# Query-bias products of a 16-head cross-attention layer: four 32-column groups and a spread through DRAM in place of a repeated 128-column weight

## The reference

```python
def _cross_attention(q_in, kv_in, wq, bq, wk, bk, wv, bv, wo, bo, bias_k, bias_v):
    b, q_len, _ = q_in.shape
    t = kv_in.shape[1]
    qh = (q_in @ wq + bq).reshape(b, q_len, H, K)
    kh = (kv_in @ wk + bk).reshape(b, t, H, K)
    vh = (kv_in @ wv + bv).reshape(b, t, H, K)
    kh = jnp.concatenate([kh, jnp.broadcast_to(bias_k, (b, 1, H, K))], axis=1)
    vh = jnp.concatenate([vh, jnp.broadcast_to(bias_v, (b, 1, H, K))], axis=1)
    scale = jnp.sqrt(jnp.asarray(K, q_in.dtype))
    logits = jnp.einsum('bqhk,bthk->bhqt', qh, kh) / scale
    weights = jax.nn.softmax(logits, axis=-1)
    ctx = jnp.einsum('bhqt,bthk->bqhk', weights, vh).reshape(b, q_len, H * K)
    return ctx @ wo + bo
```

## Time and profile before

| what | value |
|---|---|
| median of three runs | 795.99 us |
| the profiled execution | 796.76 us, of which its span is 794.8 us |
| PE busy | 697.0 us, 88% of the span |
| DVE, ACT, POOL busy | 492.8, 319.8, 318.4 us |
| chain that ended last | PE 61%, DVE 20%, DMA 5%, ACT 4%, POOL 4% |
| DMA moved | 46.70 MB, mean 59 GB/s |

### The profile page before, as it was taken

One profiled execution on the slowest core, in us unless ns is written; L12 is line 12 of the kernel. 1 busy time (PEld: TensorE's weight loads), 2 busy tenths in 40 slices (PEclk: granted clock), 3 DMA queues, 4 the chain that ended last, 5 costly groups with the idle time before them and its releaser, 6 DMA issues.

```text
span 794.8 us, 11731 instructions
## 1 busy us (share of the span) xinstructions
PE 697.0 (88%) x4432; PEld 509.8 (64%) x4432; DVE 492.8 (62%) x840; ACT 319.8 (40%) x693; POOL 318.4 (40%) x292
## 2 busy tenths in 40 slices
PE   6769989778978897699999999999998998795798
PEld 5446655447864454487757777875767897254588
DVE  4356677656555999546457674334797766498553
ACT  2044444423204777455532225652332411486311
POOL 4023444521524888453126640002675522286200
PEclk9578998999989999899999999999999999998899
DMA  5866742010006000004530000440000002000000
GB/s 174 226 161 187 215 116 46 2 35 0 1 1 211 1 1 1 2 22 163 188 106 1 1 1 19 148 152 1 0 1 1 1 1 92 15 1 1 0 27 27
DMA packets 40528, 46.70 MB, mean 59 GB/s; under 512 B 5697, under 2 KB 34970, under 8 KB 40346
## 3 DMA queue, kind: packets, MB, share of 16 engines
q1 hardware_dynamic: 38888, 44.46, 18.6%
q10 hardware_dynamic: 1586, 1.51, 0.7%
HBM read 37.72 MB, written 8.13 MB: 58 GB/s over the span
## 4 chain that ended last, share of the span: by engine, by line
PE 61%; DVE 20%; DMA 5%; ACT 4%; POOL 4%; issue 3%; ACTq 1%; SPq 1%; DVEq 0%; POOLq 0%
PE narrow_ps L510 8%; PE wide_ps L852 7%; PE wide_ps L491 6%; PE narrow_ps L887 5%; PE wide_ps L803 5%; PE wide_ps L839 3%; PE wide_ps L826 3%; PE wide_ps L543 3%; PE narrow_ps L693 3%; DVE scoresb L1376 3%; DVE mx L1385 2%; DMA wstream<-in_wqT 2%; PE wide_ps L471 2%; DVE sums L1392 2%; POOL probs L1684 2%
## 5 line engine op out<-in xcount | busy, mean ns | idle before, releaser
L1675 POOL TENSOR_TENSOR scoresb<-scoresb,mx 128x768 f32<-128x768 f32 (+1 forms) x40 | 70.7, 1769 | 152.5 <-DVE mx L1383 114.5
L1661 POOL TENSOR_TENSOR rstd<-veps,mhalf 128x1 f32<-128x1 f32 x56 | 33.2, 593 | 146.6 <-DVE veps L1304 146.6
L1051 ACT ACTIVATE probsT<-wide_ps 128x1024 f32<-128x1024 f32 x40 | 41.0, 1025 | 103.1 <-PE wide_ps L543 103.1
L1684 POOL TENSOR_TENSOR probs<-scoresb,rcp 128x1024 f32<-128x1024 f32 x40 | 78.2, 1955 | 7.0 <-DVE rcp L1393 7.0
L510 PE MATMUL narrow_ps<-wstream_r,hidden 128*128 128x256 f32 x576 | 71.9, 285 | 8.0 <-DVE hidden L1361 7.7
L510 PEld LDWEIGHTS narrow_ps<-wstream_r,hidden 128*128 128x128 f32 x576 | 70.8, 191 | 9.5 <-DVE hidden L1361 8.2
L491 PE MATMUL wide_ps<-xq_r,wstream_r 128*128 128x512 f32 x192 | 64.7, 419 | 4.8 <-issue 4.5
L543 PEld LDWEIGHTS wide_ps<-ident,probs 128*128 128x128 f32 x320 | 38.0, 146 | 46.5 <-issue 45.9
L543 PE MATMUL wide_ps<-ident,probs 128*128 128x128 f32 x320 | 44.3, 284 | 25.1 <-POOL probs L1684 23.3
L1444 DVE TENSOR_REDUCE mx<-wide_ps 128x2 f32<-128x640 f32 x64 | 49.6, 818 | 18.6 <-PE wide_ps L629 18.1
L803 PE MATMUL wide_ps<-scoresb_r,probs_r 128*128 128x256 f32 x256 | 55.7, 300 | 6.1 <-DVE vwb L1550 4.2
(11 more groups left out here) (182 smaller groups left out, 1526.3 us busy)
## 6 DMA issues: line engine op xcount, KB each, us to landing
wstream<-in_L_xattn_wk SPq DMA_DIRECT2D x8, 512.0 KB, 3.9
wstream<-in_L_xattn_wv SPq DMA_DIRECT2D x8, 512.0 KB, 5.1
wstream<-in_L_xattn_wo SPq DMA_DIRECT2D x8, 512.0 KB, 6.2
wstream<-in_wqT SPq DMA_DIRECT2D x8, 512.0 KB, 7.7
qrow<-qscratch SPq DMA_DIRECT2D x16, 192.0 KB
kscratch<-kparts SPq DMA_DIRECT2D x7, 320.0 KB, 2.4
qscratch<-qparts SPq DMA_DIRECT2D x8, 256.0 KB, 2.9
wstream<-in_L_xattn_mlp_w SPq DMA_DIRECT2D x2, 1024.0 KB, 5.3
```

The costliest lines, as they stand in the source:

```text
L1051: nc.scalar.activation(dst, src, ACT.Identity, **kw).then_inc(ring.drained[ring.slot(key)], 1)
L1675: g.tensor_tensor(s3[:, first:], s3[:, first:], mx[:, u % 3, first:].unsqueeze(2).broadcast_to([P, 16 - first, n_scores]), ALU.subtract).t ...
L1684: g.tensor_tensor(probs[:, u % 2, :].rearrange("p (h k) -> p h k", h=16), s3[:, :, 0:T], rcp[:, u % 3, :].unsqueeze(2).broadcast_to([P, 16 ...
```

## The change

The product bq times keys is issued once for a pair of heads, in the odd head, as four matmuls whose weights have 32 equal columns. Column group i (output rows 32i to 32i + 31) holds half of the keys (129 of 257, one key twice) of one head. ACT scales the 129 columns into a small row buffer. SP then stores one row of each group to DRAM (two DMAs, two rows of 129 numbers each), waits until both have landed, and loads the 514 numbers of the pair from DRAM into all 128 rows of cB with one DMA. SP does that for two pairs ahead of each weight group from g = 2 on, and for four pairs ahead of the load of the MLP's weights. DVE waits at the start of `attend2` for all eight loads in place of ACT's last two scalings. The row buffers are two; ACT waits for the store of two pairs before.

```diff
-                    bq = column(f"L2_bq{a + 1}", h)
-                    ps, filled = take_narrow(("cB", a, h))
-                    mm(ps[:, 0:NK2], bq.broadcast_to([P, P]), hb[:, 0:NK2], start=True, stop=True).then_inc(filled, 1)
-
                     if h % 2 == 1:
+                        ps, filled = take_narrow(("cB", a, h // 2))
+                        for i in range(4):
+                            g, lo = h - 1 + i // 2, i % 2 * (NK2 - HALF_KEYS)
+                            m = mm(ps[32 * i:32 * i + 32, 0:HALF_KEYS], column(f"L2_bq{a + 1}", g).broadcast_to([P, 32]),
+                                   heads[g % 4][:, lo:lo + HALF_KEYS], start=True, stop=True)
+                        m.then_inc(filled, 1)
...
+            def score_bias(a, pair):
+
+                n = 8 * a + pair
+                sp.wait_ge(*narrow.empty(("cB", a, pair)))
+                for i in range(2):
+                    lo, hi = (0, NK2 - HALF_KEYS) if i == 0 else (NK2 - HALF_KEYS, NK2)
+                    sp.dma_start(cscratch[a, 2 * pair:2 * pair + 2, lo:hi],
+                                 cbrow[n % 2][32 * i:32 * i + 65:64, 0:hi - lo]).then_inc(cb_stored[n % 2], 16)
+                sp.wait_ge(cb_stored[n % 2], 32 * (n // 2 + 1))
+                if n == 4:
+                    sp.wait_ge(xn_ready, 2 * NQ)
+                sp.dma_start(cB[:, 2 * pair:2 * pair + 2, :].rearrange("p h k -> p (h k)"),
+                             cscratch[a:a + 1, 2 * pair:2 * pair + 2, :].rearrange("a h k -> a (h k)").broadcast_to([P, 2 * NK2])
+                             ).then_inc(cb_loaded, 16)
+
             for g in range(8):
                 a, h0 = g // 4, (g % 4) * GROUP
...
                 else:
+                    for i in range(2):
+                        score_bias((g - 2) // 4, 2 * ((g - 2) % 4) + i)
                     sp.wait_ge(*wide.full(("VW", (g - 2) // 4, 2 * ((g - 2) % 4) + 1)))
...
-            sp.wait_ge(*wide.full(("VW", 1, 5)))
+            for pair in range(4, 8):
+                score_bias(1, pair)
             sp.dma_start(*halves(mlp_load(1, 0), t["L2_xattn_w_fc1"])).then_inc(load["mlp2"], 16)
...
-                    key = ("cB", a, h)
-                    act.wait_ge(*narrow.full(key))
-                    if a == 0 and h == 8:
-                        act.wait_ge(xn_ready, 2 * NQ)
-                    nc.scalar.mul(cB[:, h, :], narrow_ps[:, narrow.slot(key), 0:NK2], DH2 ** -0.5
-                                  ).then_inc(narrow.drained[narrow.slot(key)], 1)
                     if h % 2 == 1:
+                        key = ("cB", a, h // 2)
+                        n = 8 * a + h // 2
+                        act.wait_ge(*narrow.full(key))
+                        if n >= 2:
+                            act.wait_ge(cb_stored[n % 2], 32 * (n // 2))
+                        nc.scalar.mul(cbrow[n % 2], narrow_ps[:, narrow.slot(key), 0:HALF_KEYS], DH2 ** -0.5
+                                      ).then_inc(narrow.drained[narrow.slot(key)], 1)
...
                     if step == -2:
-                        for h in range(H2 - 2, H2):
-                            dve.wait_ge(*narrow.empty(("cB", a, h)))
+                        dve.wait_ge(cb_loaded, 16 * 8 * (a + 1))
```

More of the change, by code:

```diff
@@ L14 @@
 NK2 = B * T + 1
+HALF_KEYS = (NK2 + 1) // 2
 KEYS0 = S + T
@@ L241, in build @@
         cB = xq[:, 0:H2 * NK2].rearrange("p (h k) -> p h k", h=H2)
+        cbrow = [probsT[:, i, 0:HALF_KEYS] for i in range(2)]
+        cscratch = nc.dram_tensor("cscratch", (2, H2, NK2), F32).ap()
         wring = [wstream[:, i * 4096:(i + 1) * 4096].rearrange("p (m n) -> p m n", m=4) for i in range(2)]
@@ L296, in build @@
         kv_split = sem("kv_weights_split")
+        cb_stored = [sem(f"cb{i}_stored") for i in range(2)]
+        cb_loaded = sem("cb_loaded")
         stored = sem("out_stored")
```

## The result

The changed kernel took 805.14 us (median of seven runs, 802.94 to 810.28) against 795.99; the ratio is 1.0113, 95% interval 1.0082 to 1.0143: slower, inside the range and by the mechanism of the forecast, 3.6 us above the point of 801.5.

The account below looks back on a forecast made before the run. PE was taken to set the pace in precompute2, with four weight groups landing just in time or late. Delays +4.9, clock +1.7, PE's saving −1.6 gave +5.0 us: 801.5 us, 8-in-10 range 795 to 808.

Parts of the forecast that it names:

- Delay of the weights: At weight groups 2, 3, 6 and 7, SP's store, wait and load ahead of the weights cost 4.9 us together.
- D: Delay of a group's weights from SP's trip through DRAM: 1.6 us, bounds 0.9 and 3.2; 1.9 by the skill page.
- the slack of 0.83 and 0.64: At groups 3 and 6, us by which PE could have begun earlier in the kernel before, subtracted from the delay.
- The clock: PE idle 2.6 to 2.8 us at groups 2 and 7; one clock fall of the two counted, 1.7 us.
- What PE gets back: In both precompute2 stages, outside the four issue-to-first-product stretches, removed cB products less the new ones save 1.6 us.
- quad: Set of four 32-column products on 129 columns in an odd head, put at 0.38 us, between 0.29 and 0.48.
- What was called free: Last pair's cB landing by T + 3.4, before DVE's first use at T + 4.2; also later stores and MLP weights.
- I would be wrong if there were one: Sign against the forecast: DVE waiting for cB at `attend2`; a landing 0.8 us later would be felt.
- The short trip: Rival: weights delayed by 0.9 us per group, up to 1.6, and no clock fall; 795 to 799.3 us, chance 0.27.
- Late and cold: Rival: weights delayed 3.2 us, clock falls at all four groups; 812 to 813 us, chance 0.13 shared with groups in sequence.
- The saving whole: Rival: the weights' landing stays put and PE's saving of 5.7 us lands whole; about 790.5 us, chance 0.08.
- The four groups do run side by side: Rival denied this: four products in sequence cost 0.86 us, total 807 us; chance 0.13 shared with the late, cold case.

Follow-up runs that it names:

- one_row: The changed kernel, but each load writes one row of cB in place of 128 (2 KB for 263 KB); 798.79 us, ratio 1.0018.
- kept_warm: The changed kernel with 16 extra identity transposes on PE ahead of the first products of groups 2, 3 and 7; 805.83 us, ratio 1.0053.
- trip_alone: The kernel before, with its 128-column products, plus SP storing one row of each cB pair and loading it into all rows; 810.80 us, ratio 1.0174.
- the repaired versions: The changed kernel with weights issued ahead of the second pair's trip (794.15 us), with the weight-group wait cut in two (791.41), or with both (792.61).

## Why the prediction came out as it did

**Delay of the weights: right mechanism, its parts off both ways.** SP's trip was forecast to put the first issue at 1.3 us and measured 0.82 to 0.84 at all four groups: the second store landed in 1.47 us, not 1.7, and the load's issue took 0.34, not 0.5. The Trainium skill, "DMA: Bandwidth & Descriptors", section on the anatomy of one DMA, gives its fixed 2.0 us for DMAs that GpSimd issues. These were issued by SP, and the trace has 1.47 here, less even than the 1.7 that I took. That the D of 1.9 which I had worked out from the 2.0 lies near the measured one comes from the 257 KB and not from the landing. The 257 KB ahead of the weights were sized at 0.3 us and cost 10.5 − 9.4 = 1.0 or somewhat more (the landings under one_row). I had priced them at the full rate, but with them in front the first four and a half microseconds run at about three quarters of that of the earlier trace rows (mean of eleven slices 214 GB/s for 292). D came to 0.8 + 1.0 = 1.8 on the mean, forecast 1.6; by group it was 2.0, 2.9, 0.8 and 1.8. The four stretches from L847 to a group's first products grew by 2.0, 2.0, 0.1 and 1.8 us, 5.9 in all, forecast 4.9. That is D at groups 2 and 7 and D less the slack of 0.83 and 0.64 at groups 3 and 6, as the prediction had it.

**The clock: the term that was mis-sized.** I counted one fall, 1.7 us; there were three, each slower by 1.4 to 1.5 us in its products: 4.4 us. The gaps were longer than forecast (3.41 and 3.03 for 2.6 to 2.8), and group 3's also fell, since D was larger there. I had also passed over a neighbour: the prediction rests on the gap of 2.09 us behind which the clock held, but at 337.32 in the same trace it fell behind 2.08. The Trainium skill, "TensorE: Matmul & The Clock Gate", section on HAM oscillation, describes matmuls that start slow again behind each wait for a DMA; the trace agrees at three groups of four, and not at group 6 with its 1.08 us of idleness. In kept_warm, where transposes filled part of the wait, the clock held at all three places.

**What PE gets back.** Forecast 1.6 us outside the four stretches. The two profiles as they are give 8.5 = 5.9 + 4.4 − 1.8, so 1.8, but 1.2 of that is the low clock at the start of before; at an equal clock it is 9.7 = 5.9 + 4.4 − 0.6, and that 1.8 lies near the forecast is luck. A quad took 0.36 to 0.40, forecast 0.38. An even head gives 0.11, forecast 0.17, and it is ACT's emptying of slot 0 that stands in the chain, as forecast. Heads 0 and 2 of the first stage give nothing: from head 1's first product to head 4's it is 10.63 us in the changed kernel and 10.65 in trip_alone with the old products, because the split of head 4's weights (ACT, then DVE) ends last there. Inside the stretches, where I needed no number, the heads with transposes give 0.43 once the weights are in time, which helps the repaired versions beyond the 2.5 I expected of them.

So the sum was 4.9 + 1.7 − 1.6 = 5.0 us and the stages show 5.9 + 4.4 − 0.6 = 9.7. All three terms erred to the same side, the clock most: the mechanism was right and the size nearly twice the forecast, which the range was wide enough to hold.

**What was called free.** The last pair's cB lands later than I had it: with T = 406.52, the end of L847, its load was issued at T + 0.5 and took 4.5 us (group 5's weights follow 0.4 us behind it), so it landed at T + 5.0 for the forecast T + 3.4. DVE did wait for it, in the timeline of the changed kernel:

```profile
411.52 0.19 DVE L1613 SCALAR_TENSOR_TENSOR scoresb<-narrow_ps,xq 128x16 f32<-128x16 f32 x1 [6.42 <-DMA xq<-cscratch]
```

The product that it reads was there at 410.54, so the wait was 1.0 us, and I had said that I would be wrong if there were one. It cost nothing: the chain runs on PE through that time, and the stretches behind the stages are as long as before.

**Rivals.** The short trip (D 0.9, clock held) failed on the 257 KB and the clock. "Late and cold" had the clock nearly right and D too large (3.2 for 1.8). The saving whole stayed out; its turning point D = 0.8 was passed by the issue alone. The four groups do run side by side.

## What to carry to other kernels

A queue that only issues transfers has a critical path of its own: before putting a wait into it, ask what stands behind and when that is due. Here 2 KB with a round trip ahead of 2 MB made a removal of PE work a loss of 1.1%, and the same work two lines further down is a gain of 0.3%. And cut a wait by what is needed first: splitting one semaphore for four transfers into two took the trip off the path whatever its order.

## What the runs showed of the hardware that I had not expected

A gap's length alone did not tell whether the clock would fall: it fell behind 2.09 us (trip_alone), 2.33 (one_row) and 2.54 (kept_warm), and stayed up behind 2.65 (trip_alone). Behind the same 2.08 or 2.09 at the start of a stage it fell in five cases of twenty. What decides between 2.1 and 2.8 us stays open. A load of one 2 KB stretch of DRAM into 128 rows took 3.4 us to land (median of 16: 3.0 to 3.4 with nothing issued right behind it, 3.8 to 5.4 otherwise), and transfers behind it were 1.0 to 1.4 us late, more than the 0.7 of its bytes at 380 GB/s; whether the shared source or its writes are the reason was not tried.
